# A graph layer on one core: 16 edge tiles a step instead of 14

## The reference

```python
msg = relu(x[src] + edge_attr)                        # 400000 x 32
agg = segment_sum(msg, dst, num_segments=12500)
h = (1.0 + eps[0]) * x + agg
out = layernorm(x + h @ W.T + b)                      # over the 32 features, no scale, no shift
```

## Time and profile before

| | us |
|---|---|
| runs, median of three | 2125.67 |
| runs, lowest and highest | 2123.66, 2126.28 |
| the profiled execution | 2123.52 |
| its span, first to last instruction | 2121.7 |
| mean granted clock of TensorE | 0.993 of full |

### The profile page before, as it was taken

How to read it: one execution, slowest core, us unless ns; L and a number is a source line. 1 busy time by engine, 2 the same in 40 slices (tenths; PEclk the granted TensorE clock), 3 DMA queues, 4 the chain that set the end, 5 groups by cost and what they waited for, 6 DMA issues and landing times. The chain is left out here.

```text
span 2121.7 us, 126654 instructions
## 1 busy us (share of the span) xinstructions
PE 2039.3 (96%) x49730; PEld 1935.3 (91%) x49730; DVE 1687.8 (80%) x4596; ACT 1726.8 (81%) x1839; POOL 1550.5 (73%) x1570
## 2 busy tenths in 40 slices
PE   3999999999999999999999999999999999999996
PEld 2899999999999999999999999999999999999993
DVE  7888877787888888888888887778888888888874
ACT  5788888888888888888888888888888888888883
POOL 5577777777777777777777777777777777777770
PEclk9999999999999999999999999999999999999997
DMA  5565556655665655556565555555565665666551
GB/s 150 97 111 114 116 118 118 118 112 113 113 119 118 118 111 116 116 113 119 118 118 114 114 111 118 118 118 117 113 115 115 114 119 119 116 112 117 115 116 32
DMA packets 261598, 241.87 MB, mean 114 GB/s; under 512 B 115286, under 2 KB 232192, under 8 KB 261573
## 3 DMA queue, kind: packets, MB, share of 16 engines
q1 hardware_dynamic: 208395, 214.21, 41.3%
q0 software_dynamic: 50048, 25.72, 16.6%
q10 hardware_dynamic: 3130, 1.60, 0.3%
HBM read 238.52 MB, written 2.81 MB: 114 GB/s over the span
## 5 line engine op out<-in xcount | busy, mean ns | idle before, releaser
L514 POOL DMA_INDIRECT rows_all<-in_x,index x1564 | 1550.0, 991 | 515.2 <-issue 432.8
L1144 PE MATMUL found<-table,oh 128*128 128x128 bf16 x18732 | 1181.3, 221 | 25.3 <-DVE oh L738 1.5
L1144 PEld LDWEIGHTS found<-table,oh 128*128 128x128 bf16 x18732 | 1096.0, 132 | 61.8 <-ACT table L935 46.7
L1124 PE MATMUL l<-xparts,oh 128*57 128x96 bf16 x21408 | 498.4, 207 | 1.8 <-issue 0.9
L1124 PEld LDWEIGHTS l<-xparts,oh 128*57 128x57 bf16 x21408 | 467.9, 108 | 18.4 <-issue 2.9
L960 ACT ACTIVATE oh<-slots,minus_lanes 128x1824 bf16<-128x1824 f16 x223 | 403.0, 1807 | 19.6 <-DMA slots<-slot_dram 17.8
L935 ACT CAST table<-l 128x768 bf16<-128x768 f32 x446 | 355.7, 798 | 63.7 <-PE l L1124 41.2
L967 ACT ACTIVATE oh<-oh 128x1824 bf16<-128x1824 bf16 x223 | 384.5, 1724 | 0.0
L979 ACT ACTIVATE oh<-keys,minus_lanes 128x896 bf16<-128x896 f16 x223 | 232.4, 1042 | 175.5 <-PE found L1144 173.2
L753 DVE COPY_PREDICATED rows_all<-mask,found 128x224 f32<-128x224 uint16 x892 | 357.7, 401 | 8.2 <-issue 1.2
L726 DVE TENSOR_SCALAR oh<-slots,lanes 128x1824 bf16<-128x1824 f16 x446 | 302.1, 719 | 2.6 <-DMA slots<-slot_dram 2.4
(11 more groups left out here) (123 smaller groups left out, 918.5 us busy)
## 6 DMA issues: line engine op xcount, KB each, us to landing
slots<-slot_dram SPq DMA_DIRECT2D x223, 456.0 KB
msg<-in_edge SPq DMA_DIRECT2D x446, 112.0 KB
keys<-key_dram SPq DMA_DIRECT2D x223, 224.0 KB
rows_all<-in_x,index POOLq DMA_INDIRECT x1564
index<-in_src SPq DMA_DIRECT2D x223, 3.5 KB
key_dram<-key SPq DMA_DIRECT2D x223, 1.8 KB
slot_dram<-slot_row SPq DMA_DIRECT2D x223, 3.6 KB
dst_rows<-in_x ACTq DMA_DIRECT2D x1, 1562.5 KB
```

What stands on the lines that cost most here:

```text
L514: pool.indirect_dma_start(to, None, x, bass.IndirectOffsetOnAxis(indices[:, j:j + 1], 0)).then_inc(done, 16)
L1124: last = nc.tensor.matmul(l1_of(g)[half * HALF:half * HALF + CAP, :, :], oh1[:, j, b * CAP:(b + 1) * CAP], xparts[:, j * EVEN + b, :, :], ...
L1144: last = nc.tensor.matmul(found[:, t * FOUND:(t + 1) * FOUND], marks[:, t, :], table[:, b, n * FOUND:(n + 1) * FOUND],  start=(b == 0 and ...
```

## The change

Batches have 16 tiles, eight gathered and eight looked up. 3125 is 195 times 16 and 5 over, so there are 195 steps and a short batch of 5. POOL's turns have 3, 3 and 2 gathers instead of 3, 2 and 2. All sizes that follow from `LOOK` and `TILES` grow with them: the keys from 896 to 1024 columns, `ranks` from 7 x 32 to 8 x 32, `found` from 896 to 1024 columns, which is all of its two banks. `place` is no store of its own now but the store of the sources: `describe` writes the place over the source, and so takes `side` and the bits for the key from the source first. The chunks of 8 and 72 steps stay as they are.

```diff
-    LOOK = 7
-    POOLED = 7
+    LOOK = 8
+    POOLED = 8
...
-    TURNS = [(0, 3), (3, 5), (5, POOLED)]
+    TURNS = [(0, 3), (3, 6), (6, POOLED)]
...
-        place = sb("place", [P, LOOK, ROWS], I32)
...
         src_sb = sb("src_sb", [P, LOOK, ROWS], I32)
+
+        place = src_sb
...
                 own(nc.vector.tensor_tensor(bucket[:, :, some], bucket[:, :, some], t, ALU.max))
+                own(nc.vector.tensor_scalar(side[:, :, some], n, SIDE - 1, None, ALU.bitwise_and))
+                own(nc.vector.tensor_scalar(t, n, EVEN - SIDE, 4, ALU.bitwise_and, ALU.logical_shift_left))
                 own(nc.vector.tensor_scalar(place[:, :, some], n, EVEN.bit_length() - 1, None, ALU.logical_shift_right))
                 own(nc.vector.scalar_tensor_tensor(key_base[:, :, some], place[:, :, some], float(SUBS * P), place[:, :, some], ALU.is_ge, ALU.mult))
                 own(nc.vector.tensor_scalar(key_base[:, :, some], key_base[:, :, some], float(CAP - SUBS * P), 0.0, ALU.add, ALU.max))
-                own(nc.vector.tensor_scalar(t, n, EVEN - SIDE, 4, ALU.bitwise_and, ALU.logical_shift_left))
                 own(nc.vector.tensor_tensor(key_base[:, :, some], key_base[:, :, some], t, ALU.add))
-                own(nc.vector.tensor_scalar(side[:, :, some], n, SIDE - 1, None, ALU.bitwise_and))
```

## The result

The changed kernel takes 2178.35 us in the median of four runs (2177.20 to 2179.21), the kernel before 2125.24 in as many (2123.66 to 2126.28). The ratio is 1.0241, with a 95% interval of 1.0228 to 1.0253: slower by 2.4%. The forecast was 2074 us, with 2106 as its upper end. It was wrong in sign as well as in size.

A forecast was written before the change was run, and what follows sets the result against it. A loop of PE's look-ups and DVE's mask and picks was taken as the bound. 120.9 us up to look-up 6, 188 steps x 10.09 = 1896.9 and 53.0 behind gave span 2070.8; with 1.8 and 2.1 added, 2074 us, range 2063 to 2106.

The forecast's parts named there:

- The table look-ups: PE's step: table look-ups grow from 84 to 96 matmuls at 0.059 us each, +0.71 us a step.
- The other four terms: PE's step: bucket look-ups unchanged at 2.16 us, fill_slots +0.04, count_ranks +0.11, sum before the table look-up +0.17.
- The prologue: Time before the steps: larger chunks and eight rounds for seven cost 0 to 4 us, taken as +2 us.
- Rival C: POOL beside DVE: gathers delayed from about 0.46 us a step on make the kernel slower, 2151 us; chance 0.05.
- Rival A: POOL sets the step: eight gathers take 9.98 us plus delays, giving 2080, 2100 or 2110 us; beyond 2082, chance 0.25.
- POOL covered by its lead: POOL's lead in batches hides its delays, so PE's loop sets the step: 2060 to 2082 us, chance 0.66.
- the front of the sum: PE's step before the first table look-up: DVE's four picks and counts grow, +0.17 us a step.
- The window ahead of the first table look-up: PE's gap behind the fourth pick, before the first table look-up: expected near 0.25 us.
- The tail: Time behind the last bucket look-up: 51.7 us grows by 1.0 and 0.3 to 53.0 us.
- The shared store and the new order: Reordered description, with place written over the source: the order was to cost nothing.
- Both signs of being wrong: Step over 10.2 us while POOL's lead holds, or over 15 us more ahead of look-up 6, would refute the forecast.
- The lock: GpSimd and two-port DVE operations excluding each other: would give 12.6 us a step, some 2530 us; given no chance.

The follow-up runs named there:

- the mended kernel: Changed kernel with keys in two groups of four tiles (weights read 8 bytes apart) and late loads split 64 and 3: 2126.76 us, ratio 1.0034 to before.

## Why the prediction was wrong

**The table look-ups.** The step that failed is "the 84 take 2.48 + 1.17 + 1.31 = 4.96 us between starts, 0.059 each, so +0.71". I carried a duration over to a changed size because the shape in the row stayed 128x128, and didn't ask what `t=LOOK` does in the access pattern. The term measured +1.17. The other four terms held, and in a kernel with 14 bytes PE's step was 10.04 against the forecast's 10.09. The missing 0.45 a step is 85 of the 104 us.

The Trainium skill has the rule that bears on this. In SBUF — State Buffer, in the box "SBUF cachelines", it says that lines are 16 bytes, that two hits a line are needed for full bandwidth, and that a stride is free up to 8 bf16. The traces agree with 16 bytes as the place where it ends: the next load starts 56 ns later with 2, 4, 8 and 14 bytes, and 60 with 16 and 18. They disagree on 8 bf16 itself, which was not free: from 7 elements to 8 a table look-up costs 0.005 us more, 95 us in the kernel before. A single load does get longer below that, from 98 ns next to each other to 132 with 14 bytes, but the step only lost 0.10 us by it.

**The prologue.** The step that failed is "I take ends of 0 (DVE's part lies beside POOL and the loads) and 4 us". I priced DVE's larger chunks and put the loads at nothing, though the second load of the sources and that of the destinations go from 95 rows to 67. The term was +2 and measured +21 up to look-up 6. The Trainium skill (DMA: Bandwidth & Descriptors, "Why a DMA increments its semaphore by 16 and not by 1") has a transfer spread over the largest number of engines up to 16 that divides its outer sizes. By it 95 rows go over five engines, 67 over one, 64 over sixteen. The runs agree as far as times go: split in 64 and 3, the same rows are cast at 9.42 us and not at 17.74, and the first look-up starts 21 us earlier. No trace here tells the engines of a load.

**Rival C, slower.** Its sign came true by luck. Its mechanism, POOL beside DVE, didn't act in the changed kernel: with a gather fewer it takes no less time. But the doubt behind C was sound. I took 0.31 us as the most that delays reach in a step, and in the mended kernel they are 0.53, above C's threshold of 0.46.

**Rival A.** It is what would have come next. The mended kernel has the step and the start that I had forecast, or a little better, and takes 2127 and not 2074: no faster than before, and past A's dearest case of 2110. POOL covered by its lead had 0.66 of my chances and would have failed as well. The reasoning that failed is on the earlier trace rows, "so the delays go by where in DVE's step the gathers fall, and may go by it again": they came to 0.53 us a step and not to 0.1. In the kernels before and after, delays and issue fill POOL's time just to PE's step: after, 10.54 - 8 x 1.247 = 0.56 us. A POOL that keeps step with DVE's pattern while it is a little faster settles where its delays equal the difference. That is argued from the constant lead (counted as in the earlier trace rows, POOL of the kernel after has done 722 gathers, 5 + 89 x 8 + 5, when PE has done 88 bucket look-ups, and 1474, 5 + 183 x 8 + 5, when it has done 182) and not shown by a run. Its consequence was seen: such a POOL says nothing about how fast it could go.

**What held.** `fill_slots`, `count_ranks` and the front of the sum within 0.02 us each. The window ahead of the first table look-up, 0.26 for "near 0.25". The tail 2 us under its 53. The shared store and the new order at nothing. Both signs of being wrong came: a step over 10.2 while POOL's lead holds, and over 15 us more ahead of look-up 6.

**The lock.** I dismissed the Trainium skill's rule (SBUF — State Buffer, "SBUF: two separate sides") that GpSimd and certain DVE operations exclude each other, because it gave 11.3 us for a step of 9.06, and because of one gather that took 0.94 beside both slot marks. That gather started 0.02 us before the marks, and the pair of marks then took 1.38 us; in the mended kernel's row above, where they start first, it is 1.29. So the rule's "whichever starts first" agrees with the trace in one direction: a gather that starts within such an operation is held. In the other it doesn't: marks that start within a gather lose 0.1 us and not the 0.94 of the gather. What was wrong was to add all marks to the step, 2.6 us: the gathers that started within such operations lost 0.3 us a step in the kernel before.

No version here that computes everything beats the kernel before. The best is the mended one, 0.3% behind it.

## What to carry to other kernels

A tile count that turns up in a `rearrange` of an operand is a stride, and a row count that turns up in a DMA can cost more than its bytes (67 rows landed 8 us later than 95 did): before scaling a duration by a count, list every access pattern in which the count stands, and price the new one from a kernel that has it. The shape printed in a profile's row hides the stride, so an equal shape is no proof of an equal cost; and where instructions overlap, the time from start to start prices them, not the length of one. An engine whose idle gaps are all its issue time may be in step with the bound by its delays; leaving out one of its operations shows in a single run what it costs.

## What the runs showed of the hardware

- Weight loads of 128x128 bf16 for matmuls of 128 columns, by the distance of their elements in SBUF: every 56 ns (median) with 2, 4, 8 and 14 bytes, every 60 with 16 and 18. The mean length of one, at a mean granted clock of 0.99, is 98 ns (2 bytes), 115 (8), 132 (14), 146 (16). From 14 bytes to 16 a table look-up costs 0.0051 us more, from 2 to 14 about 0.001.
- A gather of 128 rows by POOL takes 0.94 us alone. In the kernel before each of the 88 over 0.97 us between 600 and 1000 us ended 0.81 to 0.82 us after the end of the DVE operation in which it started, a key mark or the addition. Picks held none.
- The kernel before took 2121 to 2122 us on two chips of the experiments and 2997, 3054 and 3055 us on three others. In a set of bucket look-ups on the latter PE stood still about three to four times, mostly for 0.6 to 1.3 us, and the mean granted clock was mostly 0.95 for 0.99. Changes cost other shares there: 16 bytes in the kernel before 0.2% and not 4.5%. A verdict of one chip doesn't carry over to such another.
